# Weighted sums of a graph attention layer with the weights as the streamed operand, and a new order of steps

## The reference

```python
h = einsum('bnd,ade->bane', x, W)                 # 12 heads of 32
th = tanh(h)
attn = (th . w_src) + (th . w_dst).T              # one number a node each, for each head
attn = where(attn >= 0, attn, 0.2 * attn)
attn = softmax(where(adj, attn, -999), axis=-1)   # 128 x 128 a head
feat_out = einsum('banm,bame->bane', attn, h) + b
feat_out = elu(feat_out, heads side by side)
gate = sigmoid(x @ H_w.T + H_b)
x = layernorm(x + gate * feat_out + (1 - gate) * x)
```

## Time and profile before

| | before |
|---|---|
| median of 3 runs | 1223.84 us (1223.67 to 1231.86) |
| the profiled execution | 1226.67 us |
| its span, first to last instruction | 1224.7 us |
| mean granted TensorE clock | 0.951 |
| TensorE busy | 1129.6 us (92%) |
| TensorE weight loads busy | 1001.1 us (82%) |
| VectorE busy | 885.6 us (72%) |
| GpSimd busy | 688.7 us (56%) |
| ScalarE busy | 621.9 us (51%) |

### The profile page before, as it was taken

One profiled execution on the slowest core, in us unless ns is written; L12 is line 12 of the kernel. 1 busy time (PEld: TensorE's weight loads), 2 busy tenths in 40 slices (PEclk: granted clock), 3 DMA queues, 4 the chain that ended last, 5 costly groups with the idle time before them and its releaser, 6 DMA issues.

```text
span 1224.7 us, 24638 instructions
## 1 busy us (share of the span) xinstructions
PE 1129.6 (92%) x7407; PEld 1001.1 (82%) x7407; DVE 885.6 (72%) x2288; ACT 621.9 (51%) x1996; POOL 688.7 (56%) x605
## 2 busy tenths in 40 slices
PE   6898999999999999999989999999999999898775
PEld 4688888888888888888878888888888888788674
DVE  2548779585976958588695958769585886957647
ACT  4546465554645556464554646455454645545221
POOL 0336566565656656565665756566564656655444
PEclk9998999989999999999999999999999999998865
DMA  6100010100000010000001001000100000000000
GB/s 170 29 8 29 20 29 14 41 6 19 28 26 28 13 41 6 19 28 26 28 13 41 6 19 28 26 28 13 41 6 19 28 26 28 13 14 8 20 1 26
DMA packets 34718, 30.94 MB, mean 25 GB/s; under 512 B 15872, under 2 KB 34688, under 8 KB 34688
## 3 DMA queue, kind: packets, MB, share of 16 engines
q1 hardware_dynamic: 34688, 30.57, 8.0%
HBM read 17.98 MB, written 12.58 MB: 25 GB/s over the span
## 4 chain that ended last, share of the span: by engine, by line
PE 62%; DVE 16%; issue 12%; ACT 7%; POOL 2%; SPq 1%; DMA 0%; DVEq 0%; ACTq 0%; POOLq 0%
PE p_bank L472 41%; PE context L620 7%; ACT probs L689 5%; DVE weights L907 5%; PE scores L533 4%; PE t_bank L609 3%; PE context L554 2%; PE t_bank L580 2%; PE t_bank L542 2%; DVE neg_max L825 1%; DVE cT L785 1%; PE t_bank L600 1%; DVE x L855 1%; DVE stats L844 1%; DVE sum L936 1%
## 5 line engine op out<-in xcount | busy, mean ns | idle before, releaser
L1010 POOL TENSOR_TENSOR w_rows<-qwT,own_head 96x1536 fp32r<-96x1536 f32 x64 | 176.1, 2751 | 187.0 <-ACT qwT L750 187.0
L907 DVE SCALAR_TENSOR_TENSOR weights<-t_bank,pqw,clip 128x128 f32<-128x128 f32 x768 | 215.0, 344 | 38.0 <-PE t_bank L609 35.6
L620 PEld LDWEIGHTS context<-h,weights 128*128 128x128 f32 x1536 | 204.4, 203 | 6.4 <-DVE weights L907 1.5
L620 PE MATMUL context<-h,weights 128*128 128x33 f32 x1536 | 199.6, 279 | 0.8 <-DVE weights L907 0.8
L689 ACT ACTIVATE probs<-masked,neg_max 128x128 f32<-128x128 f32 x384 | 148.7, 390 | 34.5 <-DVE neg_max L825 34.5
L1003 POOL TENSOR_TENSOR prod<-th,w_sd 128x768 f32<-128x768 f32 x64 | 117.0, 1828 | 86.7 <-ACT th L717 86.7
L991 POOL TENSOR_TENSOR probs<-probs,rden 128x768 f32<-128x768 f32 x64 | 98.3, 1537 | 100.1 <-DVE rden L830 100.1
L472 PE MATMUL p_bank<-w_f,cT 128*128 128x384 f32 x576 | 120.5, 354 | 13.7 <-DVE cT L785 13.7
L878 DVE TENSOR_REDUCE sd<-prod 128x24 f32<-128x768 f32 x64 | 60.6, 947 | 92.0 <-POOL prod L1003 92.0
L472 PE MATMUL p_bank<-w_g,x1T 128*128 128x384 f32 x576 | 123.6, 362 | 0.0
L472 PE MATMUL p_bank<-w_h,x1T 128*128 128x384 f32 x576 | 120.4, 355 | 2.6 <-DVE x1T L785 2.6
(11 more groups left out here) (101 smaller groups left out, 2100.8 us busy)
## 6 DMA issues: line engine op xcount, KB each, us to landing
x_in<-in_x_dram SPq DMA_DIRECT2D x16, 768.0 KB, 4.7
out_dram<-y_out SPq DMA_DIRECT2D x64, 192.0 KB, 1.9
adj_in<-in_adj_dram SPq DMA_DIRECT2D x16, 64.0 KB, 4.4
probs0T<-in_L_gnn_Wq_dram SPq DMA_DIRECT2D x1, 576.0 KB, 5.8
weights<-in_L_gnn_Wk_dram SPq DMA_DIRECT2D x1, 576.0 KB, 6.9
x_res<-in_L_gnn_Wv_dram SPq DMA_DIRECT2D x1, 576.0 KB, 7.3
probs<-in_L_gnn_Wf_dram SPq DMA_DIRECT2D x1, 576.0 KB, 7.6
x<-in_L_gnn_W_dram SPq DMA_DIRECT2D x3, 192.0 KB, 6.0
```

The costliest lines, as they stand in the source:

```text
L620: last = te.matmul(context1[:, n * (HD1 + 1):(n + 1) * (HD1 + 1)], weights[:, n, :], h[:, g % 2, n, :], start=True, stop=True)
L907: last = dve.scalar_tensor_tensor(out=weights[:, n, :], in0=src[:, i * P:(i + 1) * P], scalar=pqw[:, g % 2, 0, n:n + 1], in1=clip[:, g, :] ...
L1010: pool.tensor_tensor(w_rows[0:QW_ROWS, k % 2], over_heads(qwT[:, k % 2, 1, :].bitcast(F32), H1), per_head(own_head[:], P), ALU.mult).then_ ...
```

## The change

In layer 1's weighted sums the roles are exchanged. For each head the 32 columns of h are loaded as the operand that stays, and the head's 128 columns of weights stream past. Four heads write the four blocks of 32 partitions of `context1`, and three such rounds fill its columns 0 to 383. Beside each value matmul there is a second one, past a 128x32 block `one_hot` that has ones in a single column, which adds up the weights of the head; these sums collect in the columns 384 to 511. The sums now have the features on the partitions, so two steps are added: `sumsTo` (ACT) copies the whole bank, 128x512, to SBUF, and `sumsT` (PE) transposes it in four blocks of 128x128 into a `t_bank`. `rden1` and `f_raw` read them there.

`pv1` is one step for all 12 heads of a graph, 24 matmuls, after the last `e` of the graph; it waits for the copy `sumsTo` of the graph before, not for `f_raw`. `weights` has two buffers. The column of ones in `h` goes. `v` and `gate` wait for the low parts that they read by waits of their own. All lists of steps are written anew: of them, the diff below shows the loop's for TensorE and ScalarE, the new one for VectorE, and the beginning of ScalarE's for the first group. The lists for GpSimd and the other phases change in the same manner, in the places of steps that are otherwise the same.

```diff
--- before.py
+++ after.py
@@ -25,98 +25,98 @@
 PE_LOOP = [
-    ("v", 0), ("x1T", 0), ("qk", 0), ("qk", 1), ("x1T", 1), ("h", 0), ("gate", 0), ("qk", 2), ("qk", 3), ("qwT", 0),
-    ("h", 1), ("x1T", 2), ("qk", 4), ("qk", 5), ("wb", 0), ("gate", 1), ("s", 0), ("v", 1), ("qwT", 1), ("wb", 1),
-    ("h", 2), ("wb", 2), ("pv1", 0), ("pv1", 1), ("wb", 3), ("pv1", 2), ("wb", 4), ("s", 1), ("gate", 2), ("wb", 5),
-    ("x1T", 3), ("pv1", 3), ("s", 2), ("pv1", 4), ("h", 3), ("pT", 0), ("pv1", 5), ("pT", 1), ("s", 3), ("qwT", 2),
-    ("pT", 2), ("pv0", 0), ("v", 2), ("wb", 6), ("pT", 3), ("wb", 7), ("pv1", 6), ("pv0", 1), ("wb", 8), ("pT", 4),
-    ("pv1", 7), ("pT", 5), ("qwT", 3), ("f", 0), ("v", 3), ("pv1", 8), ("wb", 9), ("wb", 10), ("pv0", 2), ("f", 1),
-    ("wb", 11), ("pv1", 9), ("maskT", 0), ("pv1", 10), ("pT", 6), ("pv1", 11), ("xT", 0), ("pT", 7), ("f", 2),
-    ("gate", 3), ("xT", 1), ("pv0", 3), ("xT", 2), ("xT", 3), ("f", 3), ("maskT", 1),
+    ("v", 0), ("x1T", 0), ("qk", 0), ("qk", 1), ("x1T", 1), ("qk", 2), ("h", 0), ("gate", 0), ("qk", 3), ("h", 1),
+    ("qk", 4), ("qk", 5), ("qwT", 0), ("x1T", 2), ("gate", 1), ("s", 0), ("qwT", 1), ("v", 1), ("wb", 0), ("wb", 1),
+    ("s", 1), ("wb", 2), ("h", 2), ("wb", 3), ("wb", 4), ("pv1", 0), ("s", 2), ("wb", 5), ("gate", 2), ("sumsT", 0),
+    ("x1T", 3), ("pv1", 1), ("h", 3), ("pT", 0), ("pT", 1), ("pT", 2), ("pT", 3), ("pv0", 0), ("s", 3), ("sumsT", 1),
+    ("qwT", 2), ("v", 2), ("f", 0), ("qwT", 3), ("pv0", 1), ("wb", 6), ("wb", 7), ("v", 3), ("pT", 4), ("pT", 5),
+    ("wb", 8), ("pv0", 2), ("wb", 9), ("wb", 10), ("pv1", 2), ("wb", 11), ("f", 1), ("pT", 6), ("sumsT", 2),
+    ("pv1", 3), ("maskT", 0), ("pT", 7), ("f", 2), ("sumsT", 3), ("pv0", 3), ("xT", 0), ("gate", 3), ("xT", 1),
+    ("maskT", 1), ("f", 3), ("xT", 2), ("xT", 3),
 ]
 ACT_LOOP = [
-    ("x1hi", 0), ("vout", 0), ("qkout", 0), ("qkout", 1), ("hout", 0), ("pqw", 0), ("x1hi", 1), ("qwhi", 0),
-    ("qkout", 2), ("gatet", 0), ("qwTo", 0), ("qkout", 3), ("hout", 1), ("qkout", 4), ("qkout", 5), ("masks", 0),
-    ("x1hi", 2), ("pqw", 1), ("qwhi", 1), ("qwTo", 1), ("exp", 0), ("hout", 2), ("vout", 1), ("gatet", 1), ("elu", 0),
-    ("x1hi", 3), ("exp", 1), ("pqw", 2), ("pTo", 0), ("hout", 3), ("qwhi", 2), ("pTo", 1), ("qwTo", 2), ("exp", 2),
-    ("pTo", 2), ("pqw", 3), ("qwhi", 3), ("chi", 0), ("pTo", 3), ("elu", 1), ("vout", 2), ("pTo", 4), ("qwTo", 3),
-    ("pTo", 5), ("gatet", 2), ("chi", 1), ("exp", 3), ("elu", 2), ("chi", 2), ("vout", 3), ("pTo", 6), ("xhi", 0),
-    ("pTo", 7), ("xhi", 1), ("elu", 3), ("chi", 3), ("gatet", 3), ("xhi", 2), ("xhi", 3),
+    ("vout", 0), ("x1hi", 0), ("qkout", 0), ("qkout", 1), ("qkout", 2), ("hout", 0), ("x1hi", 1), ("qkout", 3),
+    ("masks", 0), ("hout", 1), ("qkout", 4), ("pqw", 0), ("qwhi", 0), ("pqw", 1), ("gatet", 0), ("qwhi", 1),
+    ("qwTo", 0), ("qkout", 5), ("x1hi", 2), ("qwTo", 1), ("gatet", 1), ("vout", 1), ("exp", 0), ("hout", 2),
+    ("sumsTo", 0), ("exp", 1), ("x1hi", 3), ("elu", 0), ("hout", 3), ("pTo", 0), ("pTo", 1), ("pqw", 2),
+    ("sumsTo", 1), ("pTo", 2), ("qwhi", 2), ("pTo", 3), ("chi", 0), ("pqw", 3), ("qwhi", 3), ("qwTo", 2), ("exp", 2),
+    ("vout", 2), ("gatet", 2), ("qwTo", 3), ("exp", 3), ("chi", 1), ("pTo", 4), ("pTo", 5), ("elu", 1), ("sumsTo", 2),
+    ("vout", 3), ("chi", 2), ("pTo", 6), ("sumsTo", 3), ("elu", 2), ("pTo", 7), ("chi", 3), ("xhi", 0), ("xhi", 1),
+    ("elu", 3), ("xhi", 2), ("xhi", 3), ("gatet", 3),
 ]
...
 DVE_LOOP = [
...
+    ("x1lo", 0), ("gsum", 0), ("x1lo", 1), ("sd", 0), ("sda", 0), ("wlog", 0), ("sd", 1), ("sda", 1), ("qwlo", 0),
+    ("wlog", 1), ("qwlo", 1), ("gsum", 1), ("x1lo", 2), ("mask", 0), ("max", 0), ("e", 0), ("e", 1), ("e", 2),
+    ("mask", 1), ("rden0", 0), ("e", 3), ("max", 1), ("e", 4), ("e", 5), ("rden1", 0), ("f_raw", 0), ("rden0", 1),
+    ("x1lo", 3), ("gsum", 2), ("sd", 2), ("sda", 2), ("wlog", 2), ("mask", 2), ("max", 2), ("sd", 3), ("sda", 3),
+    ("mixa", 0), ("qwlo", 2), ("wlog", 3), ("mixb", 0), ("rden1", 1), ("sum1", 0), ("qwlo", 3), ("clo", 0),
+    ("f_raw", 1), ("stats1", 0), ("mask", 3), ("rden0", 2), ("max", 3), ("mv1", 0), ("sum0", 0), ("e", 6), ("e", 7),
+    ("stats0", 0), ("clo", 1), ("rden0", 3), ("mv0", 0), ("e", 8), ("e", 9), ("e", 10), ("e", 11), ("mixa", 1),
+    ("sum0", 1), ("rden1", 2), ("mixb", 1), ("f_raw", 2), ("clo", 2), ("stats0", 1), ("clip", 0), ("x1", 0),
+    ("sum1", 1), ("out", 0), ("sum0", 2), ("rden1", 3), ("mv0", 1), ("f_raw", 3), ("mixa", 2), ("stats1", 1),
+    ("clo", 3), ("xlo", 0), ("mixb", 2), ("mv1", 1), ("gsum", 3), ("stats0", 2), ("x1", 1), ("xlo", 1), ("clip", 1),
+    ("mv0", 2), ("sum0", 3), ("stats0", 3), ("sum1", 2), ("xlo", 2), ("mv0", 3), ("xlo", 3), ("mixa", 3),
+    ("stats1", 2), ("out", 1), ("mv1", 2), ("mixb", 3), ("sum1", 3), ("stats1", 3), ("mv1", 3), ("x1", 2), ("out", 2),
+    ("x1", 3), ("out", 3),
 ]
...
 ACT_FIRST = [
-    ("whi", 2), ("whi", 3), ("whi", 4), ("qkout", 0), ("masks", 0), ("qkout", 1), ("qkout", 2), ("qkout", 3),
-    ("qkout", 4), ("qkout", 5), ("exp", 0), ("vout", 0), ("exp", 1), ("vout", 1), ("pTo", 0), ("pTo", 1), ("exp", 2),
...
+    ("qkout", 0), ("masks", 0), ("qkout", 1), ("qkout", 2), ("qkout", 3), ("whi", 2), ("whi", 3), ("qkout", 4),
+    ("qkout", 5), ("vout", 0), ("exp", 0), ("vout", 1), ("ghi", 0), ("exp", 1), ("pTo", 0), ("pTo", 1), ("exp", 2),
...
@@ -240,7 +240,9 @@
         clip = sb("clip", [P, GROUP, P])
         x1T = sb("x1T", [P, 2, KT, P], F32R)
         th = sb("th", [P, D])
-        h = sb("h", [P, 2, H1, HD1 + 1])
+        h = sb("h", [P, 2, D])
+        one_hot = sb("one_hot", [P, THIRDS, HD1])
+        sumsT = sb("sumsT", [P, D + P])
         gate_sum = sb("gate_sum", [P, D])
         gate_t = sb("gate_t", [P, 2, D])
         prod = sb("prod", [P, 2, D])
@@ -254,7 +256,7 @@
         qwT = sb("qwT", [QW_ROWS, 2, 2, P], F32R)
         own_head = sb("own_head", [QW_ROWS, H1])
         w_rows = sb("w_rows", [P, 2, H1, P], F32R)
-        weights = sb("weights", [P, H1, P])
+        weights = sb("weights", [P, 2, H1, P])
         rden1 = sb("rden1", [P, H1])
         f_raw = sb("f_raw", [P, D])
         f_b = sb("f_b", [P, 2, D])
...
@@ -445,7 +449,8 @@
 
 
             t_freed = {"xT": (s_xlo, GROUP), "x1T": (s_x1lo, GROUP),
-                       "qwT": (s_qwT, GROUP), "wb": (s_e, THIRDS * GROUP), "maskT": (s_mx, 2), "pT": (s_pT, 2 * GROUP)}
+                       "qwT": (s_qwT, GROUP), "wb": (s_e, THIRDS * GROUP), "maskT": (s_mx, 2), "pT": (s_pT, 2 * GROUP),
+                       "sumsT": (s_fraw, GROUP)}
             p_freed = {"qk": (s_qk, 2 * PAIRS), "v": (s_v, GROUP), "f": (s_sum0, GROUP),
                        "h": (s_h, GROUP), "gate": (s_gsum, GROUP)}
 
@@ -518,6 +523,7 @@
 
                     if phase == "first" and k == 0:
                         te.wait_ge(s_wlo, 3)
+                    te.wait_ge(s_xlo, upto(g0, GROUP, k + 1))
                     dst = bank(p_bank, p_freed, name, k, g1, phase)
                     project(dst[:, 0:D], lambda a, kt: xT[:, a, kt, k * P:(k + 1) * P],
                             lambda b, kt: w["v"][:, b, kt, :]).then_inc(pe["v"], 1)
@@ -589,6 +595,7 @@
                             lambda b, kt: w["h"][:, b, kt, :]).then_inc(pe["h"], 1)
                 elif name == "gate":
 
+                    te.wait_ge(s_x1lo, upto(g1, GROUP, k + 1))
                     dst = bank(p_bank, p_freed, name, k, g1, phase)
                     project(dst[:, 0:D], lambda a, kt: x1T[:, a, kt, :],
                             lambda b, kt: w["g"][:, b, kt, :]).then_inc(pe["gate"], 1)
@@ -611,15 +618,31 @@
                               start=True, stop=True).then_inc(pe["wb"], 1)
                 elif name == "pv1":
 
-                    g, r = divmod(k, THIRDS)
-                    te.wait_ge(s_e, upto(g1, THIRDS * GROUP, k + 1))
-                    te.wait_ge(s_h, upto(g1, GROUP, g + 1))
-
-                    wait(te, s_fraw, upto(g1, GROUP, g))
-                    for n in range(H1 // THIRDS * r, H1 // THIRDS * (r + 1)):
-                        last = te.matmul(context1[:, n * (HD1 + 1):(n + 1) * (HD1 + 1)], weights[:, n, :],
-                                         h[:, g % 2, n, :], start=True, stop=True)
+                    te.wait_ge(s_e, upto(g1, THIRDS * GROUP, THIRDS * (k + 1)))
+                    te.wait_ge(s_h, upto(g1, GROUP, k + 1))
+
+                    wait(te, s_sumsT, upto(g1, GROUP, k))
+                    if phase == "second" and k == 0:
+                        te.wait_ge(s_hot, 2)
+                    for r in range(THIRDS):
+                        for t in range(H1 // THIRDS):
+                            n = H1 // THIRDS * r + t
+                            te.matmul(context1[t * HD1:(t + 1) * HD1, r * P:(r + 1) * P],
+                                      h[:, k % 2, n * HD1:(n + 1) * HD1], weights[:, k % 2, n, :],
+                                      start=(r == 0), stop=False)
+
```

(39 more changed lines are left out.)

76 lines of the change are left out of this document (32 added, 44 removed), and 17 rows, old and new, of tables (PE_FIRST, PE_LAST).

## The result

| | before | after |
|---|---|---|
| median | 1223.81 us (1223.67 to 1231.86, 4 runs) | 1118.42 us (1116.9 to 1119.69, 4 runs) |
| the profiled execution, its span | 1226.67, 1224.7 us | 1116.9, 1114.9 us |
| mean granted clock | 0.951 | 0.987 |
| until the first x1T; 15 iterations; the rest | 68.3; 1078.3; 78.0 us | 62.7; 986.9; 65.3 us |

After stands to before as 0.9117 (95% interval 0.9089 to 0.9146). The forecast was 1190 us in a range from 1170 to 1225: the direction was right, the size about a third of the real one, and the range missed the time.

A forecast was written before the change was run, and what follows sets the result against it. TensorE was taken to bound the loop: its matmuls plus 3.26 us idle an iteration. Terms of -36 and +2 us gave -34 from the profiled 1226.7 us, so 1192.7, or 1190 us for the median; range 1170 to 1225.

The forecast's parts named there:

- the step of the sums: pv1 on TensorE: 48 records a graph, four side by side, 1.55 us a graph instead of 2.58.
- sumsT, sumsTo, the banks: New transposes 0.43 us a graph on TensorE; copy 0.69 us on ScalarE, costed at nothing; bank waits 2 us in all.
- The 2 us for banks held until `f_raw`: sumsT holds a transpose bank until VectorE has made rden1 and f_raw: 0.15 us an iteration, 2 us in all.
- The stream: TensorE's sums and new transposes: 2.58 to 1.98 us a graph, -2.4 us an iteration, -36 us over 15 iterations.
- In the loop I keep the idle time at 3.2 us an iteration: TensorE's loop idle time unchanged, as no chain feeding it gets shorter; bounds 2 and 5 us an iteration.
- the ends: First and last groups, outside the loop: both costed at nothing.
- Nothing, +-2 us: First group: six qk steps of 2.1 us on TensorE cover the moved conversions, so no change, +-2 us.
- -3 and +3: Last group: up to 1 us a graph less for three graphs, rden1 at 1216.6 instead of 1213.6 us; nothing in sum.
- Waits that grow: Rival, chance 0.14: four side by side, but loop idle time 4.5 us an iteration instead of 3.2; 1210 us.
- three side by side: Rival, chance 0.14: only three pv1 records overlap on TensorE, 2.41 us a graph with transposes; 1216 us.
- Rival 3: Chance 0.19: only two pv1 records overlap on TensorE, 3.29 us a graph with transposes instead of 2.58; 1269 us.

The follow-up runs named there:

- two_positions: The changed kernel with its sum matmuls reordered, positions 0 and 1 for all rounds, then 2 and 3: 1170.42 us, 0.9499 of before.
- before_128_columns: The kernel before, with each pv1 matmul streaming 128 columns of h instead of 33 past the same weights: 1214.94 us, 0.9871 of before.
- new_lists_old_sums: The kernel before with all lists of the changed kernel and two weights buffers, pv1 as three steps in a row: 1268.98 us, 1.0336 of before.
- old_sums_and_copy: new_lists_old_sums plus ScalarE's copy of the finished sums, for which the next pv1 waits instead of f_raw: 1255.05 us, 1.0206 of before.
- old_loop_lists: The changed kernel with the loop lists of the kernel before, sumsT and sumsTo a few steps behind pv1: 1431.6 us, 1.1637 of before.
- one_weights_buffer: The changed kernel with one weights buffer, so e waits for pv1 of the graph before: 1165.29 us, 0.9442 of before.
- sums_wait_f_raw: The changed kernel with pv1 waiting for f_raw of the graph before instead of the copy: 1150.27 us, 0.9345 of before.

## Why the prediction missed

**Right: the step of the sums.** Forecast 1.55 us a graph, measured 1.45 and 0.09 on entry. The extrapolation from `pv0` to four positions held; `two_positions` shows that it is the overlap.

**Nearly right: sumsT, sumsTo, the banks.** `sumsT` takes 0.44 us ahead of plain steps and 0.53 ahead of steps on a part of the array, on average 0.51 for 0.43. The copy takes 0.60 on ScalarE (forecast 0.69), and TensorE waits for it in the last group only. The 2 us for banks held until `f_raw` did not come: no such wait in the iteration. The stream fell by 2.7 us an iteration instead of 2.4, of which about 0.2 is half clock inside the old `pv1`: this term is worth 40 us, forecast 36.

Two executions lie 109.8 us apart and the forecast's terms were 34: 75.8 us are missing. They are 4.6 of stream, 2 of banks, 29.7 of idle time, 21 of clock, 5.6 in the first part and 12.8 in the last.

**Wrong: "In the loop I keep the idle time at 3.2 us an iteration".** It fell to 1.4 us, below the lower bound of 2, worth 30 us. The argument was that no chain feeding TensorE gets shorter. It looked at what a chain contains and not at how far ahead it may run. The two new freedoms are the second buffer and the copy; I priced the first at the 0.9 us of waits that the old trace shows for it. But the old order had been laid out around that one buffer, with `pv1` in thirds, so its cost stood nowhere as a wait. In the new order its removal costs 36 us of idle time, and the f_raw wait in place of the copy 30 us. The two overlap, since together they would be more than the 29.7 us that went. None alone is the cause: with the old sums the same freedoms and lists leave 3.3 to 4.0 us. Shown is that lists, freedoms and new sums are needed together; how far another order for the old sums would get is not.

**Missing: the clock.** The forecast called the clock close to full except in the last tenth of the span; over the 15 iterations it was 0.97. The forecast chose an iteration at 1.00 for its terms, and gave the half-clock stretches of the others no term. They cost 1.4 us an iteration outside `pv1`, 21 us.

**Wrong: the ends.** "Nothing, +-2 us" for the first group was -5.6 us, from its lists. For the last group, "-3 and +3": the end behind the last `e` did get about 3 us longer (from 13.2 us, after 1211.5, to 16.3, after 1098.6), but ahead of it 16 us went. The idle time of that part is unchanged, so it is the shorter stream and the clock, 0.77 for 0.61. `before_128_columns` took 6.7 us out of that part with neither new lists nor new sums, at the same granted clock of 0.77 (32 us of half clock for 61), which leaves 6.1 us for the rest of the change. The forecast's own terms for the end, 1211.5 + 12 x 0.21 + 0.4 + 0.69 + 0.85 + 0.2, give 1216.2 and not 1216.6, so +2.5; measured is 4.7 us from the last `e` to `rden1` for 2.1.

**Rivals.** Waits that grow and three side by side did not happen. Rival 3 rested on one streamed element a lane and cycle. Four streams of 128 columns in 0.109 us are 4.7 a ns, twice what `pv0` showed, so nothing like a common limit at 2.35 stands up to four positions. The Trainium skill ("SBUF — State Buffer", the table of path bandwidths) would have given rival 3's 1269 us; the trace has four times 65.5 KB in 0.109 us, 2400 GB/s by the operands' size, against its figure of about 614 in bf16. The Trainium skill ("TensorEngine Tiling (Array Packing)", the table of theoretical speedups) gives up to 4x for blocks of 32 or fewer columns; the trace agrees, in fp32, with four records in the 0.109 us of one. Even two positions gave 1170 us and not 1269, since the freedoms came with it.

**The clock: two kinds of falls.** They differ in what TensorE did in the 8 us (a length chosen here for looking back) before the granted clock fell to 0.5. One of each, from the kernel before and from `before_128_columns`, the 8 us and then the stretch behind them:

```profile
592.30:600.30 8.00, 8.00 (x63) 7.45 (x61) 7.13 (x20) 4.73 (x21) 4.61 (x3) 1.00 0.37 107
600.40:603.80 3.40, 3.40 (x18) 2.74 (x18) 3.33 (x10) 2.30 (x5) 3.02 (x3) 0.50 0.00 0
```

```profile
605.90:613.90 8.00, 5.73 (x46) 4.29 (x45) 7.47 (x18) 5.48 (x26) 6.75 (x6) 1.00 0.00 0
613.90:617.30 3.40, 3.40 (x21) 2.67 (x21) 1.05 (x4) 1.17 (x3) 1.60 (x2) 0.50 0.00 0
```

In the first, TensorE had no idle time at all, and 24 of its records were `pv1`; in the second it stood idle for 2.3 us. Of the 11 falls in the kernel before, seven are of the first kind. With less than 0.5 us idle and 24 or more records of `pv1` before them came also 17 of the 31 falls in `new_lists_old_sums` and 6 of the 17 in `old_sums_and_copy`. All three stream 33 columns past a 128x128 operand. The two kernels that stream 128 past it have 16 falls, those with the new sums have 48 (46 in `old_loop_lists`, 2 in `one_weights_buffer`), and each of these came after 1.7 us of idle time or more. So the half clock follows waits that lie close together with either form of the sums, and it follows the 33-column steps with no wait at all. In its iterations the kernel after has neither: none of its steps is of that kind, and no 8 us of them hold more than 0.8 us of idle time.

**Open:** why steps of 33 columns do it. The same steps stand in other iterations of the kernel before without a fall, so they are not enough by themselves. They keep the array for 2.6 us a graph; the 32-column steps past 128x32 blocks last 0.75 us and brought none. Whether the columns or the length of the step makes that difference was not told apart.

## What to carry over

A buffer or a hand-over around which an order was written shows hardly any wait: its price shows only when it is removed in the new order too, so bound the idle time by zero from below when a change gives freedom and a new order together. Give every stretch at the lower clock a term of its own, loop and ends apart, before costing instructions at full clock. And when a stage gets shorter, ask how much the next engine allows: here 0.8 us an iteration was left.

## What the hardware showed

- Four fp32 streams of 128 columns past 128x32 blocks in four column positions take the time of one, 0.109 us, at granted clock 1.00; at 0.5 they take 0.214 (eight records from 1098.68 to 1099.11).

```profile
1098.68 0.66 PE L630 MATMUL context<-weights,h 128*32 128x128 f32 x8 [1.45 <-DVE weights L934]
1099.11 0.65 PE L636 MATMUL context<-weights,one_hot 128*32 128x128 f32 x8
```

- Past such blocks the columns set the time (8 records: 0.06 us at 32 columns, 0.22 at 128); past a 128x128 operand 33 and 128 columns cost the same 0.1 us a record (16 records in 1.70 us with either).
- The granted clock can fall while TensorE is busy without a gap: seven times in the kernel before, after 8.00 us busy of 8.00. With the same lists, the same wait for `f_raw` and 50 us of idle time in 15 iterations it was 0.93 with the old sums (`new_lists_old_sums`) and 1.00 with the new ones (`sums_wait_f_raw`).
